# Four graph layers on one core: the sage layer's products moved behind the second layer's sums

## The chip, the cores and the metric

The kernel runs on one core of one Trainium2 chip. The metric is the device time of one execution in microseconds (us), and a lower time is better. The engines are named as in the profile: PE is TensorE (PEld its weight loads), DVE is VectorE, ACT is ScalarE, POOL is GpSimd, SP is SyncE, which here only starts transfers.

## The reference, cut to what matters

Eight graphs (B = 8) of N = 2048 nodes with F = 128 features go through four layers. Each layer is fed h, the normalised and rectified x, and its result is added to x.

```python
# layer 0: graph attention, 8 heads, then a second attention layer over its result
att = softmax(where(adj > 0, leaky_relu(f1_i + f2_j), NEG)); xc = elu(att @ h)      # 8 heads
att2 = softmax(where(adj > 0, leaky_relu(g1_i + g2_j), NEG)); x = x + elu(att2 @ (xc @ W2)) + h
# layer 1 ("sage"): the greatest feature of each node's neighbours
h = relu(layernorm(x))
neigh_agg = where(mask[..., None], h[:, None], -1e30).max(axis=2)                   # h itself where there is none
o = h @ W_self + b_self + neigh_agg @ W_neigh + b_neigh
x = x + relu(layernorm(o) * gamma + beta)
# layer 2: graph attention with 4 heads ("gat_mid"); layer 3: a mean over neighbours and two products
```

## The kernel before, in words

Nodes lie in T = 16 tiles of 128 partitions. One graph after the other goes through the stages, but two graphs are in flight, since the sage layer's maxima need a gather that takes long. For graphs b = 0 to 7 the order, written out by hand in `pipeline`, is: load and heads of 0; `beside(0, None)`; load and heads of 1; then six times `beside(b + 1, b)`, `middle(b)`, `last_layer(b, b + 2)`, `heads_of(b + 2)`; then `beside(7, 6)`, `middle(6)`, `last_layer(6)`, `beside(None, 7)`, `middle(7)`, `last_layer(7)`. Every engine runs its own program through the same order and waits on semaphores.

`heads_of` is layer 0's first attention (8 heads, LA). `beside(b, other)` holds two things: the second attention layer of graph b (LB), and the sage layer of the graph before it (other = b - 1). `middle` is layer 2 (LC) and `last_layer` is layer 3, beside which the next graph is loaded.

The gather of graph b is POOL's: it fetches rows of a table in memory by lists of neighbours (`table`, one indirect transfer for each of 8 neighbours of a tile, line 552), keeps the greatest (lines 535 to 538), and writes `Agg` (line 596). It starts when SP has stored h of graph b as the table (line 452), which SP does after norm 1, and after the gather of graph b - 1 has ended (the semaphore `maxima`, line 614). The table store of graph b thus needs, in this order: LB's preparation (`prepare`), its sums (`sums` on PE, line 1386, fed by DVE's products of line 908 through `weigh`), the second layer's `finish` on DVE (nine operations, lines 991 to 1007, with an exponential on ACT between, `elu_exp`), `statistics(1)` on DVE, and norm 1 on ACT (line 635, 16 instructions).

The sage layer of the graph before stands in the same stage. PE first waits for `maxima` (`sage_arrived`). For each of 8 pairs of tiles PE turns four blocks (lines 1343 and 1344), ACT copies them (line 718, `sage_operands`), PE multiplies (line 1355), and DVE adds the row of biases (line 1180, `sage_sums`) and takes statistics (line 1187). These steps stand between the 16 steps of LB's sums: after step 1 PE runs `sage_arrived`, and steps 2 to 9 have a product each behind them. When they are done, norm 4 (ACT), `joined` (DVE, three operations and `statistics(2)`) and norm 2 (ACT) follow, then DVE's `finish`. The list of one tile of neighbours (three parts of `list_tile`: lines 1053, 1077, 1067) is also made between steps 0 to 2 of the sums.

A few lines say it best, on PE and on DVE:

```python
for jb in range(T):                                  # sums, PE
    ...
    ins.then_inc(s["pe"], 1)
    if other is not None:
        sage_step(other, jb)                         # jb == 1: waits for maxima
...
if other is not None:                                # beside, DVE, after weigh(...)
    joined(other)
if b is not None:
    finish(LB, b, lone)
    statistics(1, b, X)
```

Of the kernel before, what the change touches and what calls it, by code (L numbers as in the profile page):

```python
# [31 lines left out]
ACT = mybir.ActivationFunctionType  # L32
# [31 lines left out]
def build(nc, x, adj, W1, a1, W2, a2, Wself, bself, Wneigh, bneigh, gamma, beta, WC, aC, W3, B3, out):  # L64
    B, N, F = x.shape
    T = N // P
    LA = Layer("gat_heads", W1.shape[0], W1.shape[2], 1)
    LB = Layer("gat_out", 1, F, W1.shape[0] * W1.shape[2] // P)
# [16 lines left out]
    with ExitStack() as ctx:  # L85
# [182 lines left out]
        def plain(eng):  # L268

            eng.wait_ge(ready, 1)  # L270
# [355 lines left out]
        def _(act):  # L626
# [84 lines left out]
            def sage_operands(b):  # L711

                s = M["sage"]
                with act.Fori(0, T // 2) as tt:
                    plain(act)
                    act.wait_ge(s["T"], b * T + tt * 2 + 2)
                    act.wait_ge(s["W"], b * T + tt * 2 + 2)
                    act.activation(hT[:, :, :, :], ps[:, 6, :].rearrange("p (u k c) -> p u k c", u=2, k=2),  # L718
                                   ACT.Copy).then_inc(s["hT"], 2)
# [60 lines left out]
            def beside(b, other):  # L780
                if b is not None:
                    prepare(LB, b)
                if other is not None:
                    sage_operands(other)
                    norm(4, other, Y, Y, ACT.Identity)
                    norm(2, other, X2, Hn2, ACT.Relu)
                if b is not None:
                    elu_exp(LB, b, 0)
                    norm(1, b, X, Hn, ACT.Relu)
# [40 lines left out]
        def _(dve):  # L830
# [148 lines left out]
            def finish(L, hn, lone):  # L979

                s, C = S[L], L.C
                v = Chain(dve, s["pv"], (hn + 2) * POST[L], POST[L])
# [13 lines left out]
                v(dve.tensor_tensor(Z[:, full * w:], Z[:, full * w:], ps[:, full, 0:T * C - full * w], ALU.add))  # L996
                v(dve.reciprocal(rden[:, :], zt[:, :, L.D]))
                v(dve.tensor_tensor(o, o, rden[:, :].rearrange("p (t o) -> p t o", o=1).broadcast_to([P, T, L.D]), ALU.mult))
                v(dve.tensor_scalar(E, o, 0.0, None, ALU.min))
                plain(dve)  # L1000
                dve.wait_ge(s["e"], hn + 1)
                v(dve.scalar_tensor_tensor(E, o, 0.0, E, ALU.max, ALU.add))

                plain(dve)
                dve.wait_ge(h0_in, hn * 16 + 16)
                v(dve.scalar_tensor_tensor(Hn[:, :, :], E, -1.0, Hn[:, :, :], ALU.add, ALU.add))
                v(dve.tensor_tensor(X[:, :, :], X[:, :, :], Hn[:, :, :], ALU.add))
                v.end()

# [173 lines left out]
            def sage_statistics(b, p):  # L1183
                plain(dve)
                dve.wait_ge(M["sage"]["ev"], b * T + (2 * p + 4))
                for t in (2 * p, 2 * p + 1):
                    dve.bn_stats(stats[:, t, :], Y[:, t, :]).then_inc(ln[4]["st"], 1)

            def beside(b, other):

                rest_of = []
                between = [] if other is None or b is None else list(zip((0, 1, 2), list_tile(b, LIST_LB)))
                if other is not None:
                    for p in range(T // 2):
                        between.append((p + 4, lambda p=p: sage_sums(other, p)))
                        between.append((p + 5, lambda p=p: sage_statistics(other, p)))
                    between.append((T // 2 + 4, lambda: rest_of.append(deviations(4, other))))
                    between.append((T // 2 + 5, lambda: rest_of[0]()))
                if b is None:
                    for at, work in sorted(between, key=lambda part: part[0]):  # L1200
                        work()
                else:
                    prepare(LB, b)
                    weigh(LB, 0, (b + 1) * 16, slice(0, 1), b, between)
                if other is not None:
                    joined(other)
                if b is not None:
                    finish(LB, b, lone)


                    statistics(1, b, X)

# [67 lines left out]
        def _(pe):  # L1280
# [83 lines left out]
            def sage_step(b, jb):  # L1364

                if jb == 1:
                    sage_arrived(b)
                if 2 <= jb < T // 2 + 2:
                    sage_product(b, jb - 2)
                if 1 <= jb < T // 2 + 1:  # L1370
                    sage_turned(b, jb - 1)

            def sums(L, hn, other):

                s = S[L]
                if other is not None:

                    plain(pe)
                    pe.wait_ge(s["hsc"], hn + 1)
                for jb in range(T):  # L1380
# [8 lines left out]
                    if other is not None:  # L1389
                        sage_step(other, jb)  # L1390
# [109 lines left out]
            def beside(b, other):  # L1500
                if b is None:
                    for jb in range(T // 2 + 2):
                        sage_step(other, jb)
                    return
                prepare(LB, b, xc, None)
                plain(pe)
                pe.wait_ge(S[LB]["v"], (b + 1) * PREP_CHAIN)
                sums(LB, b, other)
# [36 lines left out]
```

## Time and profile before

| | us |
|---|---|
| median of 3 runs | 9122.6 (9110.27 to 9135.99) |
| the profiled execution's own time | 9111.52 |
| its span, first to last instruction | 9109.8 |
| busy: DVE, PE, POOL, PEld, ACT | 5894.4, 5148.5, 5128.1, 4779.8, 4402.1 |
| mean granted TensorE clock, as a share of full speed | 0.781 |

Busy time is the sum of an engine's instructions; a share over the whole span mixes stages with different limits. A row of a timeline gives start, duration, engine, line, operation, operands and in brackets how long the engine had been idle and what ended that. "x16" means that sixteen like instructions in a row are merged. A row of stretches gives for each engine the busy time and in parentheses the number of instructions.

### The profile page before, as it was taken

How to read it: one execution, taken by the hardware profiler on the slowest of the kernel's cores; microseconds unless marked ns; L12 is line 12 of the kernel's file. 1: busy time of each engine (PE TensorE's matmuls, PEld its weight loads, DVE VectorE, ACT ScalarE, POOL GpSimd, SP SyncE). 2: the span in 40 equal slices, each digit the busy share in tenths (PEclk: the TensorE clock that was granted, in tenths of full speed). 3: DMA queues.
4: the chain of work that ended last, by engine and by line, in shares of the span. 5: the costliest groups of instructions: out<-in, count | busy, mean ns of one | idle time of the engine just before them, and what ended most of it. 6: DMA issues, size and time to landing. Idle time of an engine off the chain costs nothing.

```text
span 9109.8 us, 178961 instructions
## 1 busy us (share of the span) xinstructions
PE 5148.5 (57%) x60584; PEld 4779.8 (52%) x60584; DVE 5894.4 (65%) x7002; ACT 4402.1 (48%) x3608; POOL 5128.1 (56%) x5234
## 2 busy tenths in 40 slices
PE   3673750365765668365865667556845667362026
PEld 3672750364755557363865567555745567361025
DVE  5874860386867788486867687687847688581024
ACT  5644730165635566165735566356715566160034
POOL 0004777377764677377764677276764677377630
PEclk9885875687877878687987888788877888686568
DMA  2114332234332533135322433234322433132210
GB/s 99 43 34 124 66 66 25 46 69 113 61 63 65 122 65 80 19 76 133 67 62 66 119 66 83 58 75 101 69 48 66 120 65 80 54 55 58 23 26 29
DMA packets 307180, 629.05 MB, mean 69 GB/s; under 512 B 113553, under 2 KB 165906, under 8 KB 270610
## 3 DMA queue, kind: packets, MB, share of 16 engines
q0 software_dynamic: 91936, 161.87, 16.9%
q1 hardware_dynamic: 212354, 456.38, 14.2%
q8 instruction: 581, 9.52, 0.4%
q14 instruction: 149, 1.22, 0.0%
q10 hardware_dynamic: 2160, 0.06, 0.0%
HBM read 506.89 MB, written 111.15 MB: 68 GB/s over the span
## 4 chain that ended last, share of the span: by engine, by line
POOL 20%; issue 16%; DVE 14%; PE 13%; DMA 8%; ACT 4%; POOLq 2%; DVEq 2%; ACTq 1%; SPq 0%
DMA G<-table,idx 6%; POOL G L552 6%; POOL best L552 5%; PE ps L1413 4%; POOL best L538 4%; PE ps L1386 3%; PE ps L1415 2%; POOL best L535 2%; DVE keys L1077 2%; POOL G L535 2%; ACT Pbuf L689 1%; PE ps L1438 1%; DVE key L1067 1%; POOL best L537 1%; ACT Hn L689 1%
## 5 line engine op out<-in xcount | busy, mean ns | idle before, releaser
L552 POOL DMA_INDIRECT G<-table,idx x1416 | 1502.7, 1061 | 508.5 <-issue 452.7
L1415 PE MATMUL ps<-Hn,AT 128*128 128x99 bf16 x12288 | 1774.5, 216 | 0.0
L1415 PE MATMUL ps<-X,AT 128*128 128x99 bf16 x12288 | 1735.0, 214 | 52.6 <-issue 52.6
L544 POOL DMA_DIRECT2D idx<-lists x433 | 259.3, 599 | 2445.9 <-issue 1964.9
L689 ACT ACTIVATE Hn<-Rb,q 128x2048 int8<-128x2048 f32 x768 | 1485.4, 1988 | 86.6 <-PE ps L1415 82.1
L689 ACT ACTIVATE Pbuf<-Rb,q 128x2048 int8<-128x2048 f32 x768 | 1487.8, 1987 | 18.2 <-PE ps L1415 15.6
L552 POOL DMA_INDIRECT best<-table,idx x1024 | 1093.7, 1068 | 319.4 <-issue 309.3
L1415 PEld LDWEIGHTS ps<-X,AT 128*128 128x128 fp8e4 x12288 | 1243.2, 101 | 57.6 <-issue 57.6
L1415 PEld LDWEIGHTS ps<-Hn,AT 128*128 128x128 fp8e4 x12288 | 1256.5, 102 | 0.0
L1413 PE MATMUL ps<-X,Hn 128*128 128x198 bf16 x6144 | 933.6, 268 | 567.6 <-DVE Hn L937 358.6
L1413 PE MATMUL ps<-Hn 128*128 128x198 bf16 x6144 | 960.3, 272 | 433.0 <-DVE Zs L957 236.0
L1413 PEld LDWEIGHTS ps<-X,Hn 128*128 128x128 fp8e4 x6144 | 650.4, 106 | 594.0 <-issue 578.1
L1413 PEld LDWEIGHTS ps<-Hn 128*128 128x128 fp8e4 x6144 | 659.8, 107 | 474.5 <-issue 454.4
L1413 PE MATMUL ps<-Hn,Pbuf 128*128 128x198 bf16 x6144 | 833.9, 252 | 75.9 <-DVE Pbuf L937 75.6
L1413 PE MATMUL ps<-X,Pbuf 128*128 128x198 bf16 x6144 | 821.9, 251 | 28.7 <-DVE Pbuf L937 28.7
L908 DVE SCALAR_TENSOR_TENSOR Pbuf<-Rb,q,AT 128x2048 f32<-128x2048 f32 x128 | 303.7, 2374 | 803.0 <-PE ps L1386 781.7
L937 DVE SCALAR_TENSOR_TENSOR Hn<-Hn,AT 128x512 int32<-128x512 int32 x768 | 638.7, 860 | 219.3 <-ACT Hn L689 155.4
L718 ACT ACTIVATE hT<-ps 128x512 f32<-128x512 f32 x64 | 38.2, 597 | 1515.8 <-PE ps L1344 1515.8
L937 DVE SCALAR_TENSOR_TENSOR Pbuf<-Pbuf,AT 128x512 int32<-128x512 int32 x768 | 668.0, 899 | 137.7 <-ACT Pbuf L689 104.7
L1077 DVE MAX8 keys<-key 128x8 f32<-128x2056 f16 x305 | 701.2, 2299 | 33.8 <-DVE key L1067 7.8
L1343 PE MATMUL ps<-ident,Hn 128*128 128x128 f32 x128 | 34.5, 293 | 1146.3 <-POOLq L614 1096.9
L1413 PEld LDWEIGHTS ps<-Hn,Pbuf 128*128 128x128 fp8e4 x6144 | 606.9, 99 | 89.3 <-issue 86.9
(186 smaller groups left out, 11171.7 us busy)
## 6 DMA issues: line engine op xcount, KB each, us to landing
Rb<-in_adj SPq DMA_DIRECT2D x128, 1024.0 KB, 6.3
Rb<-rrows SPq DMA_DIRECT2D x104, 1024.0 KB, 6.3
bytes_A<-A SPq DMA_DIRECT2D x128, 256.0 KB
bytes_AT<-AT SPq DMA_DIRECT2D x128, 256.0 KB
AT<-bytes_AT SPq DMA_DIRECT2D x128, 256.0 KB, 3.6
AT<-bytes_A SPq DMA_DIRECT2D x128, 256.0 KB, 4.6
G<-table,idx POOLq DMA_INDIRECT x1416
h<-Hn SPq DMA_DIRECT2D x16, 1024.0 KB, 4.1
```

Source lines behind the costliest of these rows:

```text
L535: v(pool.tensor_tensor(b, b, a, ALU.subtract))
L537: v(pool.tensor_scalar(b, b, 3.0e38, 0.0, ALU.min, ALU.max))
L538: v(pool.tensor_tensor(a, a, b, ALU.add))
L544: pool.dma_start(idx[:, slot, :], lists[bass.ds(r, 1)].rearrange("o p k -> (o p) k")).then_inc(idx_in[slot], 16)
L552: pool.indirect_dma_start(out=dst[:, k, :], out_offset=None, in_=table, in_offset=bass.IndirectOffsetOnAxis(ap=idx[:, slot, k:k + 1], axis ...
L689: act.activation(marks[(u * T + jb) % RING].bitcast(I8), Rb[:, u, :], ACT.Sign, bias=q[:, jb, hs], scale=-1.0).then_inc(s["sg"], 1)
L908: dve.scalar_tensor_tensor(tiles_P[jb % 2], Rb[:, slot, :], q[:, jb, h], AT[:, jb, :], ALU.max, ALU.mult).then_inc(s["p"], 1)
L937: dve.scalar_tensor_tensor(marks[k % RING], marks[k % RING], NO_SIGN, A32, ALU.bitwise_and, ALU.bitwise_and).then_inc(s["p"], 1)
L1077: dve.max(keys8[:, :], key[:, :]).then_inc(found, 1)
L1386: ins = pe.matmul(ps[:, i // L.per_bank, c0:c0 + L.width], tiles_P[jb % 2][:, i * P:(i + 1) * P], rhs, start=(jb == 0 and i % L.per_bank = ...
L1413: pe.matmul(both[:, :, 0:G], greater[:, at], v.rearrange("p (g x) -> p g x", g=2), start=first, stop=False, skip_group_check=True)
L1415: ins = pe.matmul(both[:, 0, 0:G], A8[:, jb, at], v[:, 0:G], start=False, stop=jb == T - 1, skip_group_check=True)
```

## The change

On PE the sage layer's steps leave the loop of LB's sums and follow it as a block of their own, `sage`, which waits for the maxima and then turns and multiplies pair after pair. On DVE, `finish` gets a list `between`: after its third operation and after each later one it takes one `sage_sums` out of the list. The sage statistics are no longer taken pair by pair; `statistics(4)` takes them together, after `statistics(1)`, and `joined` comes last. On ACT the eight copies stand around the second layer's exponential, four ahead of it and four behind, then norm 1, then norm 4 and norm 2. The copies are written out where they were a loop. The list of a tile is made behind steps 1 to 3 in place of 0 to 2. SP's program is as before.

```diff
 act:
-            def sage_operands(b):
-                with act.Fori(0, T // 2) as tt:
+            def sage_operands(b, part):
+                for p in part:
...
                 if b is not None:
                     prepare(LB, b)
                 if other is not None:
-                    sage_operands(other)
+                    sage_operands(other, range(T // 4))
+                if b is not None:
+                    elu_exp(LB, b, 0)
+                if other is not None:
+                    sage_operands(other, range(T // 4, T // 2))
+                if b is not None:
+                    norm(1, b, X, Hn, ACT.Relu)
+                if other is not None:
                     norm(4, other, Y, Y, ACT.Identity)
                     norm(2, other, X2, Hn2, ACT.Relu)
-                if b is not None:
-                    elu_exp(LB, b, 0)
-                    norm(1, b, X, Hn, ACT.Relu)
 dve:
-            def finish(L, hn, lone):
+            def finish(L, hn, lone, between):
+                waiting = list(between)
+                def beside_it():
+                    if waiting:
+                        waiting.pop(0)()
...
                 v(dve.tensor_tensor(Z[:, full * w:], Z[:, full * w:], ps[:, full, 0:T * C - full * w], ALU.add))
+                beside_it()
                 v(dve.reciprocal(rden[:, :], zt[:, :, L.D]))
+                beside_it()
...
                 v(dve.tensor_tensor(X[:, :, :], X[:, :, :], Hn[:, :, :], ALU.add))
+                beside_it()
                 v.end()
+                while waiting:
+                    beside_it()
...
+                products = [] if other is None else [lambda p=p: sage_sums(other, p) for p in range(T // 2)]
...
                     prepare(LB, b)
-                    weigh(LB, 0, (b + 1) * 16, slice(0, 1), b, between)
+                    weigh(LB, 0, (b + 1) * 16, slice(0, 1), b,
+                          () if other is None else list(zip((1, 2, 3), list_tile(b, LIST_LB))))
+                    finish(LB, b, lone, products)
+                    statistics(1, b, X)
                 if other is not None:
+                    plain(dve)
+                    dve.wait_ge(M["sage"]["ev"], other * T + (T + 2))
+                    statistics(4, other, Y)
                     joined(other)
-                if b is not None:
-                    finish(LB, b, lone)
-                    statistics(1, b, X)
 pe:
-            def sage_step(b, jb):
-                if jb == 1:
-                    sage_arrived(b)
-                if 2 <= jb < T // 2 + 2:
-                    sage_product(b, jb - 2)
-                if 1 <= jb < T // 2 + 1:
-                    sage_turned(b, jb - 1)
+            def sage(b):
+                sage_arrived(b)
+                for p in range(T // 2):
+                    sage_turned(b, p)
+                    sage_product(b, p)
...
                     ins.then_inc(s["pe"], 1)
-                    if other is not None:
-                        sage_step(other, jb)
...
-                sums(LB, b, other)
+                sums(LB, b)
+                if other is not None:
+                    plain(pe)
+                    pe.wait_ge(S[LB]["hsc"], b + 1)
+                    sage(other)
```

## Rows read from the trace of the kernel before

**Rows 1.** Waits, longest in total: us in total, times, longest.

```profile
PE ps L1343 <- POOLq L614: 1096.9, 6, 463.0
```

**Rows 2.** Stretches from the end of a gather to the next table store.

```profile
1676.00:1790.60 114.60, 65.39 (x554) 64.81 (x555) 69.63 (x101) 34.22 (x65) 0.00 (x0) 0.77 0.00 2
2704.00:2818.30 114.30, 65.12 (x554) 64.54 (x555) 69.63 (x101) 34.23 (x65) 0.00 (x0) 0.77 0.00 2
3754.90:3869.40 114.50, 65.31 (x554) 64.73 (x555) 69.63 (x101) 34.23 (x65) 0.00 (x0) 0.77 0.00 1
4747.50:4862.40 114.90, 65.63 (x554) 65.05 (x555) 69.64 (x101) 34.22 (x65) 0.00 (x0) 0.77 0.01 2
5708.00:5833.00 125.00, 66.89 (x561) 65.87 (x561) 83.54 (x111) 34.22 (x65) 0.00 (x0) 0.77 0.01 1
6797.80:6913.20 115.40, 66.15 (x554) 65.57 (x555) 69.62 (x101) 34.23 (x65) 0.00 (x0) 0.77 0.01 2
7819.50:7937.80 118.30, 65.56 (x554) 65.05 (x555) 69.65 (x101) 34.21 (x65) 0.00 (x0) 0.76 0.00 1
```

**Rows 3.** Stretches, middle to second layer's sums; last: one where PE waits.

```profile
1825.30:2647.00 821.70, 559.16 (x6912) 515.98 (x6912) 642.22 (x730) 507.51 (x375) 588.83 (x588) 0.83 0.40 82
2854.10:3661.20 807.10, 555.77 (x6911) 512.96 (x6911) 638.08 (x726) 508.05 (x374) 576.94 (x575) 0.84 0.38 83
3904.30:4694.80 790.50, 557.56 (x6912) 513.89 (x6912) 632.56 (x714) 507.19 (x375) 578.32 (x576) 0.84 0.40 85
4896.90:5698.20 801.30, 555.51 (x6912) 511.88 (x6912) 624.20 (x726) 506.60 (x375) 581.02 (x580) 0.84 0.37 84
5867.70:6690.30 822.60, 562.75 (x6912) 518.21 (x6912) 649.85 (x738) 507.02 (x375) 584.58 (x579) 0.83 0.39 82
6947.60:7759.10 811.50, 558.16 (x6912) 514.99 (x6912) 634.32 (x718) 507.10 (x375) 583.87 (x585) 0.84 0.38 83
1313.00:1676.00 363.00, 0.76 (x7) 0.57 (x6) 15.34 (x10) 0.00 (x0) 258.65 (x298) 0.51 0.24 25
```

**Rows 4.** Timeline of the first handover, 1676 to 1826 us.

```profile
1676.48 0.47 PE L1343 MATMUL ps<-ident,Hn 128*128 128x128 f32 x1 [362.73 <-POOLq L614]
...
1753.63 2.31 DVE L991 TENSOR_TENSOR Pbuf<-lone,hsum 128x2064 f32<-128x2064 f32 x1 [0.18 <-DVE small L858]
...
1769.13 2.29 DVE L1007 TENSOR_TENSOR X<-X,Hn 128x2048 f32<-128x2048 f32 x1
...
1782.17 7.31 ACT L635 ACTIVATE Hn<-X,small  x16 [0.91 <-DVE small L858]
...
1790.63 0.83 SPq L452 DMA_DIRECT2D table<-Hn  x1
...
1804.08 2.36 DVE L892 TENSOR_TENSOR WHbuf<-WHbuf,d 128x2112 f32<-128x2112 f32 x1
...
1818.22 0.71 DVE L923 TENSOR_TENSOR Zs<-WHbuf,q 128x528 f32<-128x528 f32 x1 [11.78 <-DMA AT<-bytes_AT]
...
1825.28 7.66 ACT L689 ACTIVATE Hn<-Rb,q 128x2048 int8<-128x2048 f32 x4
```

**Rows 5.** Timeline of the last sage layer, which runs alone.

```profile
8754.63 0.45 PE L1343 MATMUL ps<-ident,Hn 128*128 128x128 f32 x1 [462.98 <-POOLq L614]
...
8775.53 0.43 DVE L1180 TENSOR_TENSOR xcbuf<-ps,rowsb 128x256 f32<-128x256 f32 x1 [1.33 <-PE ps L1355]
...
8779.43 7.18 ACT L635 ACTIVATE xcbuf<-xcbuf,small  x16 [1.05 <-DVE small L858]
```

**Rows 6.** Timeline rows of the second layer's sums, in three graphs.

```profile
634.31 59.91 PE L1386 MATMUL ps<-WHbuf,Pbuf 128*128 128x129 f32 x512 [5.18 <-DVE Pbuf L908]
...
4712.21 2.35 DVE L908 SCALAR_TENSOR_TENSOR Pbuf<-Rb,q,AT 128x2048 f32<-128x2048 f32 x1 [0.39 <-DVE found_idx L1082]
...
5721.23 4.62 DVE L908 SCALAR_TENSOR_TENSOR Pbuf<-Rb,q,AT 128x2048 f32<-128x2048 f32 x2 [0.38 <-DVE found_idx L1082]
...
5723.73 6.24 PE L1386 MATMUL ps<-WHbuf,Pbuf 128*128 128x129 f32 x32 [8.45 <-DVE Pbuf L908]
```

More of the change, by code:

```diff
@@ L709, in heads @@
                     elu_exp(LA, b * LA.H + LA.H - 1, LA.H - 1)
-            def sage_operands(b):
+            def sage_operands(b, part):
                 s = M["sage"]
-                with act.Fori(0, T // 2) as tt:
+                for p in part:
                     plain(act)
-                    act.wait_ge(s["T"], b * T + tt * 2 + 2)
-                    act.wait_ge(s["W"], b * T + tt * 2 + 2)
+                    act.wait_ge(s["T"], b * T + (p * 2 + 2))
+                    act.wait_ge(s["W"], b * T + (p * 2 + 2))
                     act.activation(hT[:, :, :, :], ps[:, 6, :].rearrange("p (u k c) -> p u k c", u=2, k=2),
@@ L1002, in finish @@
                 v(dve.scalar_tensor_tensor(E, o, 0.0, E, ALU.max, ALU.add))
+                beside_it()
                 plain(dve)
@@ L1006, in finish @@
                 v(dve.scalar_tensor_tensor(Hn[:, :, :], E, -1.0, Hn[:, :, :], ALU.add, ALU.add))
+                beside_it()
                 v(dve.tensor_tensor(X[:, :, :], X[:, :, :], Hn[:, :, :], ALU.add))
+                beside_it()
                 v.end()
+                while waiting:
+                    beside_it()
             def heads(L, b, lone, lists=None):
@@ L1181, in sage_sums @@
                                   rowsb[:, 0:1, :].broadcast_to([P, 2, F]), ALU.add).then_inc(M["sage"]["ev"], 2)
[L1183 to L1187, printed above, removed]
-            def beside(b, other):
-                rest_of = []
-                between = [] if other is None or b is None else list(zip((0, 1, 2), list_tile(b, LIST_LB)))
-                if other is not None:
[L1194 to L1198, printed above, removed]
+            def beside(b, other):
+                products = [] if other is None else [lambda p=p: sage_sums(other, p) for p in range(T // 2)]
                 if b is None:
-                    for at, work in sorted(between, key=lambda part: part[0]):
+                    for work in products:
                         work()
@@ L1362, in sage_arrived, with sums @@
                 pe.wait_ge(x1_in, (b + 1) * 32)
-            def sage_step(b, jb):
-                if jb == 1:
-                    sage_arrived(b)
-                if 2 <= jb < T // 2 + 2:
-                    sage_product(b, jb - 2)
-                if 1 <= jb < T // 2 + 1:
-                    sage_turned(b, jb - 1)
-            def sums(L, hn, other):
+            def sage(b):
[3 more added lines that the diff above has]
+                    sage_product(b, p)
+            def sums(L, hn):
                 s = S[L]
-                if other is not None:
-                    plain(pe)
-                    pe.wait_ge(s["hsc"], hn + 1)
                 for jb in range(T):
@@ L1388, in sums @@
                     ins.then_inc(s["pe"], 1)
-                    if other is not None:
-                        sage_step(other, jb)
             def head(L, hn, u):
@@ L1501, in beside @@
                 if b is None:
-                    for jb in range(T // 2 + 2):
-                        sage_step(other, jb)
+                    sage(other)
                     return
@@ L1507, in beside @@
                 pe.wait_ge(S[LB]["v"], (b + 1) * PREP_CHAIN)
-                sums(LB, b, other)
+                sums(LB, b)
+                if other is not None:
+                    plain(pe)
+                    pe.wait_ge(S[LB]["hsc"], b + 1)
+                    sage(other)
             def middle(b, alone):
```

## The prediction

> **What bounds the kernel now.** I read the waits first, then the stretches around the point where one gather ends and the next begins, then the timeline of one such point. PE waits 1096.9 us in six places for the semaphore with which POOL reports a gather's end, 463.0 us of it in the last [rows 1]. So the gather is late wherever PE reaches it. The stretches from a gather's end to the next table store, seven of them, are 114.3 to 125.0 us long, and POOL does nothing in them (0.00, x0) [rows 2]. The gathers fill the time between: from table store to end they take 2704.0 - 1790.6 = 913.4, then 936.6, 878.1, 845.6, 964.8, 906.3 and, from 7937.8 to 8754.6, 816.8 us [rows 2, 5]. From the first end (1676.0) to the last (8754.6) pass 7078.6 us, and this is a plain loop: gather, handover, gather.
>
> The other engines have a loop of their own through the same point. From the first mark of the middle layer (1825.3) to the first step of the next second-layer sums (2647.0) pass 821.7 us, then 807.1, 790.5, 801.3, 822.6, 811.5 [rows 3]. Then they wait: sums begin at 2647.0 and the gather ends at 2704.0, so 57.0 us, and likewise 93.7, 52.7, 9.8, 107.6 and 60.4 us in the five stages after [rows 2, 3]. In the fourth of them the two loops are almost level. This slack is what the change can use up, and no more.
>
> **The handover after the change.** Only the sage products and `finish` stand between a gather's end and the statistics that lead to the table. Where the sage layer runs alone, its eight products are evicted 8775.53 + 0.43 - 8754.63 = 21.3 us after PE goes on [rows 5]. `finish` takes 1771.42 - 1753.63 = 17.8 us by itself [rows 4]. Both run on DVE in turns: the least is 21.3 (`finish` fits between the products), the most 39.1 (no overlap). DVE has only 8 x 0.43 us of the products, the rest of their time is spent on PE and ACT, so the value lies near the low end; since `finish`'s exponential now stands between ACT's fourth and fifth copy and delays the fifth product, I take 26. From `finish`'s end to norm 1's start pass 1782.17 - 1771.42 = 10.75 us, and the table store is issued 1790.63 - 1782.17 = 8.46 later [rows 4], together 19.2. The change adds waits for the products on DVE. Queued behind them are the rest of `finish`, statistics(1), and so norm 1 and the table store; all of these stood behind the maxima before too, so nothing new is held by a late gather. So the table goes out 26 + 19.2 = 45.2 us after the gather's end, where it now takes 114.3 to 125.0 [rows 2]. SP's program is the same; its two stores ahead of the table are in the 8.46.
>
> The gather also loses quiet time. In 363.0 us in which the others stand still POOL runs 298 instructions, 0.821 per us; in 821.7 loaded us 588, 0.716 per us [rows 3]: the same work takes 14.7% longer. A gather's end now ran quiet for 10 to 108 us, of which the first 20 or so hold the list of a tile; 14.7% of the rest is 0 to 13 us. I add 8 us to each gather but the last, whose end is quiet in both kernels. The bounds are 0 and 13.
>
> The Trainium skill says that GpSimd shares its SBUF interfaces with VectorE and contends with Vector instructions that have two SBUF inputs (GPSIMD Engine Reference, section 8, Key points). The trace agrees: 0.821 against 0.716 instructions per us [rows 3]. If that rule alone held, the move of more two-input DVE work beside the gather would speak against the change; it is the rival "slower gather" below.
>
> **The other loop after the change.** From the same release: 26 us to `finish`'s end. Then statistics(1) 10.75, statistics(4) another 10.75 (norm 1's 7.31 runs on ACT beside it), norm 4 7.3, `joined`'s three operations 3 x 2.33 = 7.0, statistics(2) 10.8, norm 2 7.3; then the middle layer's preparation as before, 1806.44 - 1789.48 = 17.0; then the first splits and the first mark, 1825.28 - 1818.22 = 7.1 [rows 4]. The sum behind `finish` is 78.0; with 1.4 for a gather that now runs beside it, 79.4. Before, DVE stood 11.78 us for AT ahead of the splits, which began 1818.22 - 1790.63 = 27.6 us after the table store that SP issues ahead of AT's transfers [rows 4]. Now 70.9 - 19.2 = 51.7 us lie between the two, so this wait is covered; if it is not, it costs up to 11.8 a stage. The release thus stands 26 + 79.4 = 105.4 us ahead of the first mark, where it was 1825.3 - 1676.0 = 149.3 [rows 3].
>
> What this loop gains there it pays at the sums. They cost little of it now, since they ran after the gather's end; they now stand wholly ahead of the products. In two graphs, begun at 4694.8 and 5698.2, DVE's product for step 3 started 17.4 and 23.0 us later, behind one and two further rounds of the list [rows 3, 6]. With the list one step later, one more product (2.3) comes ahead: step 4 can start some 22.2 and 27.8 us after the first. Then twelve steps on PE: the first after a stall 6.24, the others (59.91 - 6.24) / 15 = 3.58 each [rows 6], 45.6 in all. So 67.8 and 73.4, mean 70.6, and 0.8 until DVE is as far as it is in the late-gather case (`finish`'s first three operations against PE's first product). The least is 59.9, with the list hidden [rows 6]; the most has every step at 6.24, below.
>
> A turn of the gather's loop is now 45.2 + 8 + gather, of the other loop 105.4 + 71.4 + stretch of rows 3. The longer one counts:
>
> | to end of gather | gather's loop | other loop | taken | before |
> |---|---|---|---|---|
> | 1 | 966.6 | 998.5 | 998.5 | 1028.0 |
> | 2 | 989.8 | 983.9 | 989.8 | 1050.9 |
> | 3 | 931.3 | 967.3 | 967.3 | 992.6 |
> | 4 | 898.8 | 978.1 | 978.1 | 960.5 |
> | 5 | 1018.0 | 999.4 | 1018.0 | 1089.8 |
> | 6 | 959.5 | 988.3 | 988.3 | 1021.7 |
> | 7 | 862.0 | none | 862.0 | 935.1 |
>
> The sums are 6802.0 after and 7078.6 before: 276.6 us less. The last sage layer loses its interleaved statistics: norm 4 began 8779.43, and will begin 8775.96 + 10.75 = 8786.7, 7.3 later [rows 5]. The first graphs, up to 1676.0, are as before; the unrolled copies on ACT and the register work for DVE's added waits are costed at nothing, since the waits for PE cover them (at 0.2 us each, uncovered, 1.6 a stage). Net 276.6 - 7.3 = 269 us. The profiled execution's own 9111.5 becomes 8842; the median before is 11.1 above that execution, so from 9122.6 I forecast 8850 us.
>
> **Rivals.** *The sums are hidden anyway* (the other loop never binds): all seven turns by the gather's loop sum to 6626, 453 less, or 8677 us. For it: the loop has slack in every stage. Against it: each slack shrinks by the 69 us that the handover gives up and the 71 that the sums take, and gets back 44 at the mark and 8 from the longer gather, so by 88; of the six only 93.7 and 107.6 outlast that.
>
> *The sums run at the lower clock.* PE comes to them after pauses, and such a step takes 6.24, not 3.58; the granted clock is 0.51 where PE waits and 0.83 in loaded stretches [rows 3, 6]. All twelve steps at 6.24 cost 29.3 more, and the second column's turns sum to 6953 with the last: 9005 us. Against it: the sixteen steps of the first graph, also begun after a pause, take 59.91, or 3.74 each on average [rows 6]. The Trainium skill has TensorE at 1.2 GHz after idleness and at 2.4 GHz after sustained activity (TensorE: Matmul & The Clock Gate, Part 1); by it, too, only the beginning is slow.
>
> *Slower gather.* If the gather, with DVE busy at all times beside it, takes 10% more, the turns sum to 7207 and the time is 9258 us. The point from which it decides is 7% to 8%: at 7% the time is about 9096, at 8% 9150, where it becomes slower. For it: 14.7% between quiet and loaded. Against it: the gathers are loaded for most of their length already.
>
> *Nothing moves.* `finish` still waits for the maxima through its first product, so the table can't be stored before they are there; if the turns of DVE, PE and ACT wait for each other at every product, the handover stays near 115 and the time near 9123. Against it: 39.1 us is the sum of both without any overlap.
>
> **Chances.** Forecast 0.75, hidden sums 0.07, lower clock 0.06, slower gather 0.07, nothing moves 0.05. A measurement of this kernel can tell about 0.3%, 27 us, from no change. Faster by that: 0.88; within it 0.05; slower 0.07. The forecast's own range: `finish` at 21.3 and sums at 59.9 give some 80 less, `finish` at 39.1 in seven handovers 92 more, so 8770 to 8943. Leaving out hidden sums, slower gather and nothing moves (0.19), the range reaches to the lower clock: 8770 to 9010.
>
> **What would show it.** In the profile after, the gather's end to the table store should take about 45 us where the gather is late and PE's wait for it should fall from 1096.9 to about 770: some 300 in the first, 440 in the last, and the rest in one or two between. Of the middle five handovers, three or four should have PE not waiting at all, with the maxima 10 to 90 us before the end of the sums. The sums should take 68 to 74 from first to last step, the first mark should follow the release by about 105, and the gathers should be 0 to 13 us longer. I am wrong if the stretches of rows 3 change by more than 1%, if the handover is above 60, or if a gather is over 3% longer.

## The result, and the profile after

The changed kernel takes 8874.44 us (median of 4, 8863.03 to 8889.48) where the kernel before takes 9119.47 beside it: a ratio of 0.972, 95% interval 0.969 to 0.975. The forecast was 8850, its range 8770 to 9010. The profiled execution after took 8871.89, its span is 8870.2, so 239.6 less than the span before, where the prediction's sum has 269 less. The change does what was forecast; in the profiles, 30 us of the gain are missing.

The page after, first lines (engine, busy us, share of the span, instructions):

```profile
span 8870.2 us, 179248 instructions
...
PE 5220.8 (59%) x60584; PEld 4827.2 (54%) x60584; DVE 5925.3 (67%) x7002; ACT 4381.6 (49%) x3594; POOL 5220.3 (59%) x5234
```

Its waits (us in total, times, longest), to be read beside [rows 1]:

```profile
DVE xcbuf L1199 <- PE ps L1364: 841.7, 49, 452.1
...
PE ps L1352 <- POOLq L614: 770.9, 3, 453.2
```

PE's wait for the maxima falls from 1096.9 us in six places to 770.9 in three, which is the forecast's 770. That the sum fits so closely is luck in part: the first gather's wait is 311.9 (some 300 were forecast), the last one's 453.2 (440), and the one between them 5.8 (30). DVE's 841.7 us for the sage products are no new bound: 768 of them are these same three waits, since DVE waits behind PE.

The stretches from a gather's end to the next table store, in the columns of [rows 2]:

```profile
1687.70:1730.30 42.60, 14.68 (x96) 12.36 (x96) 24.81 (x56) 15.49 (x27) 0.00 (x0) 0.74 0.01 2
2637.10:2738.30 101.20, 67.43 (x519) 64.42 (x517) 64.54 (x76) 15.50 (x27) 0.00 (x0) 0.81 0.01 2
3682.90:3732.10 49.20, 23.70 (x96) 20.20 (x96) 24.79 (x56) 15.61 (x27) 0.00 (x0) 0.50 0.01 3
4646.20:4706.40 60.20, 33.02 (x224) 30.14 (x222) 36.49 (x62) 15.61 (x27) 0.00 (x0) 0.73 0.01 2
5534.40:5683.80 149.40, 98.06 (x710) 93.05 (x710) 94.21 (x116) 22.20 (x41) 0.00 (x0) 0.75 0.05 17
6654.60:6700.90 46.30, 17.95 (x110) 15.40 (x109) 29.66 (x59) 15.49 (x27) 0.00 (x0) 0.71 0.01 3
7623.00:7669.30 46.30, 17.17 (x96) 14.70 (x96) 26.04 (x57) 15.50 (x27) 0.00 (x0) 0.65 0.00 2
```

Two kinds stand here. Four handovers are 42.6 to 49.2 us long: the gather is late, or within some 5 us of the end of the sums, and only products, `finish`, statistics(1) and norm 1 stand behind it. In the second, fourth and fifth POOL is done first and waits until the sums end, in the fifth for 101.7 us. There PE's instruction count (x710) shows what it is still doing: all of the sums. This is the other loop. The third is the longest of the four late ones: over it, after a pause of PE of 5.75 us, the granted clock is 0.50, the lower of the two levels, and PE's 96 instructions take 23.70 us. The first, after a pause of 311.9, has 0.74 and 14.68; why the two differ is not shown. Before, the handovers stood at 0.76 to 0.77 [rows 2], with the sums between the products.

The second layer's sums, from their first step to their last:

```profile
2624.00:2692.90 68.90, 63.26 (x514) 62.72 (x515) 47.35 (x24) 0.00 (x0) 11.83 (x10) 0.91 0.01 1
3604.70:3677.60 72.90, 61.30 (x512) 60.68 (x512) 54.08 (x28) 0.00 (x0) 59.21 (x42) 0.90 0.17 22
4594.80:4660.40 65.60, 61.14 (x514) 60.79 (x515) 45.96 (x24) 0.00 (x0) 43.91 (x29) 0.95 0.10 13
5564.40:5636.10 71.70, 61.56 (x514) 61.21 (x515) 49.61 (x29) 0.00 (x0) 0.00 (x0) 0.90 0.01 1
6581.60:6656.20 74.60, 62.27 (x514) 61.73 (x515) 54.26 (x29) 0.00 (x0) 60.08 (x44) 0.91 0.10 15
7553.00:7619.40 66.40, 61.80 (x512) 61.28 (x512) 46.88 (x24) 0.00 (x0) 54.76 (x38) 0.94 0.10 17
```

They take 65.6 to 74.6 us, at a granted clock of 0.90 to 0.95, so near the upper of the two levels. Call the later of the gather's end and the end of the sums the release. The first handover after its release, in the timeline:

```profile
1688.19 0.47 PE L1352 MATMUL ps<-ident,Hn 128*128 128x128 f32 x1 [311.92 <-POOLq L614]
...
1692.22 0.42 DVE L1199 TENSOR_TENSOR xcbuf<-ps,rowsb 128x256 f32<-128x256 f32 x1 [311.08 <-PE ps L1364]
...
1721.86 7.32 ACT L635 ACTIVATE Hn<-X,small  x16 [0.93 <-DVE small L862]
...
1730.34 0.84 SPq L452 DMA_DIRECT2D table<-Hn  x1
1732.11 7.16 ACT L635 ACTIVATE xcbuf<-xcbuf,small  x16 [0.96 <-DVE small L862]
...
1790.39 3.88 ACT L689 ACTIVATE Hn<-Rb,q 128x2048 int8<-128x2048 f32 x2
```

Norm 1 starts 34 us after the release, the table goes out at 42.6, and norm 4 of the sage layer (the second L635 row) runs behind it; the middle layer's first mark (L689) follows at 102.7. From there to the next sums, in the columns of [rows 3]:

```profile
1790.40:2624.00 833.60, 565.04 (x6912) 520.31 (x6912) 656.35 (x730) 506.81 (x375) 599.15 (x606) 0.82 0.38 81
2799.10:3604.70 805.60, 558.30 (x6911) 514.67 (x6911) 638.97 (x726) 507.27 (x375) 579.93 (x584) 0.84 0.38 83
...
5745.10:6581.60 836.50, 555.64 (x6911) 512.72 (x6911) 656.50 (x738) 507.44 (x375) 601.52 (x599) 0.83 0.39 81
```

All six are 833.6, 805.6, 802.7, 797.0, 836.5 and 792.5 us, +11.9 to -19.0 against [rows 3] and 13 us more in sum.

Where the 239.6 us come from follows from the ends of the gathers (1687.7, 2637.1, 3682.9, 4646.2, 5534.4, 6654.6, 7623.0, 8504.4) and the table stores between them, measured in both profiles and set beside the prediction's terms:

| part of the span | before | after | change | predicted |
|---|---|---|---|---|
| up to the first gather's end | 1676.0 | 1687.7 | +11.7 | 0 |
| seven stretches from gather to table | 817.0 | 495.2 | -321.8 | -324.6 |
| seven gathers, table to end | 6261.6 | 6321.5 | +59.9 | +48 |
| behind the last gather | 355.2 | 365.8 | +10.6 | +7.3 |
| sum | 9109.8 | 8870.2 | -239.6 | -269.3 |

This follows the gather alone. Where the sums end last, a longer gather only shortens the wait in the next stretch, so a row here is not yet a cost.

### The profile page after: what moved, and what is told of

It is laid out like the page before. It is cut to its first block and busy times, and to the rows that moved or that the text cites. A ratio compares the mean times of both kernels' runs of the same rounds, so it can differ in the third digit from the quotient of the medians.

```text
span 8870.2 us, 179248 instructions
## 1 busy us (share of the span) xinstructions
PE 5220.8 (59%) x60584; PEld 4827.2 (54%) x60584; DVE 5925.3 (67%) x7002; ACT 4381.6 (49%) x3594; POOL 5220.3 (59%) x5234
## 5 line engine op out<-in xcount | busy, mean ns | idle before, releaser
L1416 PE MATMUL ps<-X,AT 128*128 128x99 bf16 x12288 | 1742.1, 215 | 48.2 <-issue 48.2
L689 ACT ACTIVATE Hn<-Rb,q 128x2048 int8<-128x2048 f32 x768 | 1484.7, 1987 | 89.6 <-PE ps L1416 86.0
L689 ACT ACTIVATE Pbuf<-Rb,q 128x2048 int8<-128x2048 f32 x768 | 1487.8, 1987 | 15.1 <-PE ps L1416 11.9
L552 POOL DMA_INDIRECT best<-table,idx x1024 | 1130.0, 1104 | 318.2 <-issue 309.0
L941 DVE SCALAR_TENSOR_TENSOR Pbuf<-Pbuf,AT 128x512 int32<-128x512 int32 x768 | 644.8, 868 | 147.4 <-ACT Pbuf L689 114.8
L1414 PEld LDWEIGHTS ps<-X,Pbuf 128*128 128x128 fp8e4 x6144 | 601.9, 98 | 30.1 <-issue 29.5
L1439 PE MATMUL ps<-WHbuf,AT 128*128 128x385 bf16 x2048 | 390.1, 352 | 351.3 <-ACT WHbuf L813 351.3
```

Source lines behind the costliest of these rows:

```text
L552: pool.indirect_dma_start(out=dst[:, k, :], out_offset=None, in_=table, in_offset=bass.IndirectOffsetOnAxis(ap=idx[:, slot, k:k + 1], axis ...
L689: act.activation(marks[(u * T + jb) % RING].bitcast(I8), Rb[:, u, :], ACT.Sign, bias=q[:, jb, hs], scale=-1.0).then_inc(s["sg"], 1)
L941: dve.scalar_tensor_tensor(marks[k % RING], marks[k % RING], NO_SIGN, A32, ALU.bitwise_and, ALU.bitwise_and).then_inc(s["p"], 1)
L1414: pe.matmul(both[:, :, 0:G], greater[:, at], v.rearrange("p (g x) -> p g x", g=2), start=first, stop=False, skip_group_check=True)
L1416: ins = pe.matmul(both[:, 0, 0:G], A8[:, jb, at], v[:, 0:G], start=False, stop=jb == T - 1, skip_group_check=True)
L1439: ins = pe.matmul(ps[:, 4 + u, 0:3 * F + 1], A8[:, k, (tt * 2 + u) * P:(tt * 2 + u + 1) * P], PS3[:, k, 0:3 * F + 1], start=k == 0, stop=k ...
```

## The experiments

The first theory is that of the prediction: two loops meet at the release, and both parts of the change are needed, the early table for the gather's loop and the sums ahead for the other. The rivals: one part alone brings it all; what counts is that products and `finish` alternate, or that they do not; and, for the missing 30 us, either the stages' own work or a gather held up by DVE. Each ratio is to the kernel before, beside it on the same chip.

**The early table alone.** On the kernel before, the sage layer stays between the steps of the sums; only the order behind them changes.

```diff
-                if other is not None:
-                    joined(other)
                 if b is not None:
                     finish(LB, b, lone)
                     statistics(1, b, X)
+                if other is not None:
+                    joined(other)
```

ACT has norm 2 behind norm 1 to match.

> The kernel before with only the order changed behind the sums: finish, statistics(1) and norm 1 come ahead of joined and norm 2; the sage steps stay between the steps of the sums. Two-loop theory (the turns are set by the gather with its handover, or by the other engines' loop with the sums, whichever is longer): the handover falls from 114.6 to about 100 (63.3 of sums, 17.8 of finish, 19.2 to the table), seven times 14 us, so about 9020 us against 9119. Rival (the gain comes only from the second layer's sums no longer waiting for the maxima): no change, 9119.

9084.87 us, ratio 0.995 (0.992 to 0.997). The first handover:

```profile
1676.80:1777.50 100.70, 63.45 (x544) 63.26 (x544) 64.39 (x81) 25.65 (x46) 0.00 (x0) 0.81 0.01 2
```

The handovers shorten as expected, to about 100 us (124.3 in the fifth), 88 us less in seven. But the gathers take 44 us more in sum (6305.4 against 6261.6) and the stretch behind the last one 8, so the span is only 36 us shorter where 100 were expected, though here not one step of the sums has moved ahead of a gather's end. Work that stood in the handover, where POOL is idle, now runs beside the next gather. The prediction gave this nothing.

**The sums ahead alone.** On the changed kernel, the table again comes last.

```diff
                     finish(LB, b, lone, products)
-                    statistics(1, b, X)
                 if other is not None:
                     ...
                     statistics(4, other, Y)
                     joined(other)
+                if b is not None:
+                    statistics(1, b, X)
```

ACT has norm 4 and norm 2 ahead of norm 1.

> The changed kernel with joined, norm 4 and norm 2 put back ahead of statistics(1) and norm 1; the sums still stand ahead of the sage products. Two-loop theory: the handover grows from about 45 to about 81 (statistics, norm 4 and joined come into it), the other loop gets about 10 shorter; the turns then are mostly the gather's and the time is about 8980. Rival (only the sums' place counts): 8874, as the changed kernel. Together with e1 this splits the gain: 100 us for the table alone, 140 for the sums alone, 245 for both.

9054.44 us, 0.991 (0.988 to 0.994).

```profile
1690.10:1771.00 80.90, 21.17 (x106) 17.50 (x107) 38.61 (x86) 31.53 (x63) 0.00 (x0) 0.56 0.00 1
```

DVE's waits for AT, before and here (the changed kernel has none):

```profile
DVE Zs L923 <- DMA AT<-bytes_AT: 78.7, 7, 12.1
```

```profile
DVE Zs L927 <- DMA AT<-bytes_AT: 75.4, 7, 13.3
```

Where the gather is late the handover is 81 to 84 us, as expected; the release to the first mark is 115 to 120 us, not the 95 expected. Norm 1 now stands ahead of the middle layer's copies on ACT, which begin 79 to 83 us behind the release (77 to 84 in the changed kernel), so the 10 us are not gained. And the wait for AT is back, 10.8 us a stage, since SP issues AT's transfers behind the table store, which again goes out late: an early table also covers this wait. The time is some 74 us above the 8980 expected. So the parts alone bring 0.5% and 0.9%, together 2.8%: more than their sum. That one part brings it all is refuted. Its gathers, 6360.8 us in sum, are longer than in either kernel; why, these runs don't tell.

**No turns.** All eight products ahead of `finish`.

```diff
-                    finish(LB, b, lone, products)
+                    for work in products:
+                        work()
+                    finish(LB, b, lone, ())
```

ACT has all eight copies ahead of `elu_exp`.

> The changed kernel with all eight sage_sums ahead of the first operation of finish, and all eight copies ahead of the exponential. Two-loop theory: 21.3 us of products and 17.8 of finish then stand one behind the other, about 39 in place of 24 to 31, in both loops, so seven turns of about 12 us: 8960. Rival (the products' round trips set that stretch whatever stands between them): 8874.

8971.64 us, 0.982 (0.980 to 0.984), so 1% more than the change.

```profile
3706.40:3765.50 59.10, 15.47 (x96) 13.06 (x96) 30.00 (x59) 15.61 (x27) 0.00 (x0) 0.66 0.01 2
```

The release to `finish`'s end takes 36.8 to 40 us (48.2 in the first), near the prediction's bound without overlap of 39.1, where the changed kernel takes 24.0 to 30.6. The seven turns take 11 us more on average, 77 of the 90 us by which the span is longer (8960.0 against 8870.2). The rival, for which 8874 would stand, is refuted.

**Longer sums.** Behind each product DVE takes one more maximum, whose result nobody uses.

```diff
+                    if jb < T:
+                        dve.max(hpart[:, 136 + 8 * jb:144 + 8 * jb], iota[:, :])
```

> The changed kernel with one more DVE operation of about 2.3 us (a maximum over one tensor, whose result nobody reads) behind each of the 16 products of the sums, so that the sums take about 19 us more. Two-loop theory: 13 to 26 us more in each of the six turns of the loop (the slack there is at most 15), about 100 in all, so about 8978. Rival (the sums are hidden behind the gather): 8874.

9002.19 us, 0.984 (0.978 to 0.990).

```profile
1317.60:1408.40 90.80, 65.46 (x512) 62.99 (x512) 86.78 (x44) 0.00 (x0) 74.00 (x53) 0.89 0.16 18
```

The sums take 83.6 to 95 us, 15 to 20 more, and the span is 115 us longer: 25 up to the first gather's end, where two graphs' sums are longer too, and 90 in the turns. Five of the first six turns are 15 to 23 us longer; the fifth, for which 13 to 26 were expected too, only 0.9. So the sums are on the path, and the rival that they are hidden anyway is refuted.

**A shorter gather.** The last comparison over the eight neighbours is left out.

```diff
-                for width in (4, 2, 1):
-                    greater(v, best[:, 0:width, :], best[:, width:2 * width, :])
+                pool.sem_inc(tree, TREE - 1)
+                v.n = TREE - 1
```

> The changed kernel whose gather leaves out the last comparison over the eight columns (nine operations of POOL for each tile, about 7.5 us, so about 120 to 130 us a graph); Agg then holds the first column only. Two-loop theory: only the first gather, the last one and two turns that are level gain, about 260 us, so about 8610. Rival (the gather sets every turn): all eight gathers gain, about 1000 us, so about 7870.

8483.36 us, 0.927 (0.922 to 0.932); the profile's span is 393 us below the change's. The two loops as I had put them gave 8610, so the gain is some 127 us larger than that; the gather setting every turn would have given 7870. From the first mark to the next sums:

```profile
1668.20:2462.40 794.20, 554.23 (x6912) 511.68 (x6912) 617.50 (x730) 506.92 (x375) 489.98 (x471) 0.84 0.40 85
2632.50:3420.50 788.00, 553.02 (x6911) 510.90 (x6911) 608.80 (x726) 506.13 (x375) 509.53 (x488) 0.84 0.42 87
...
5513.60:6319.00 805.40, 554.43 (x6911) 512.04 (x6911) 627.00 (x738) 506.88 (x375) 517.13 (x502) 0.84 0.42 85
```

The gathers are 123 to 155 us shorter each, and in all six stages between, the sums now end 119 to 207 us behind the gather. So the other loop alone sets the turns there, and only the first gather (the first mark comes at 1668.2, not 1790.4) and the last count in full: 122 + 130 us. The remainder is the surprise: the other loop's stretches are shorter too, 130 us in sum. DVE runs the same 730 instructions in 617.50 us instead of 656.35, with 22% fewer POOL instructions beside it (471 against 606). So POOL slows DVE.

**A product with one input.** The second layer's product leaves out the factor AT and so reads one tensor in place of two; one takes 1.29 us in place of 2.35.

```diff
-                    dve.scalar_tensor_tensor(tiles_P[jb % 2], Rb[:, slot, :], q[:, jb, h], AT[:, jb, :],
-                                             ALU.max, ALU.mult).then_inc(s["p"], 1)
+                    dve.tensor_scalar(tiles_P[jb % 2], Rb[:, slot, :], q[:, jb, h], 1.0,
+                                      ALU.max, ALU.mult).then_inc(s["p"], 1)
```

> The changed kernel whose product for the second layer's sums reads one tensor in place of two (the mask AT is left out of it). In the changed kernel's trace a POOL operation that meets such a product takes about 2 us more, and gathers that end beside the sums are about 18 us longer there. If it is the second tensor that holds POOL up: POOL runs about 0.8 instructions per us beside the sums in place of 0.58 to 0.62, and the time falls by 20 to 40 us. If any DVE work does: the rate stays near 0.6.

8814.03 us, 0.963 (0.958 to 0.968). The first graph's sums beside the gather, in the change and here:

```profile
1301.60:1376.30 74.70, 61.54 (x512) 60.80 (x512) 54.15 (x28) 0.00 (x0) 59.50 (x46) 0.89 0.18 22
1376.30:1687.00 310.70, 0.00 (x0) 0.00 (x0) 4.76 (x3) 0.00 (x0) 221.38 (x255) 0.51 0.23 24
```

```profile
1306.60:1377.30 70.70, 62.16 (x512) 61.79 (x512) 39.13 (x28) 0.00 (x0) 54.03 (x50) 0.90 0.23 24
```

In the change POOL runs 46 instructions in 74.7 us, 0.616 per us, and behind the sums 255 in 310.7, 0.821. With the shorter product it is 50 in 70.7, 0.707. I had expected 0.8 if only a second tensor counts and 0.6 if the number of inputs does not matter. It is between, and the timeline shows why:

```profile
7519.56 0.94 POOL L552 DMA_INDIRECT best<-table,idx  x1 [0.30 <-issue]
7520.81 1.47 POOL L552 DMA_INDIRECT best<-table,idx  x1 [0.30 <-issue]
...
7520.88 2.48 DVE L912 TENSOR_SCALAR Pbuf<-Rb,q 128x2048 f32<-128x2048 f32 x2 [0.38 <-PE ps L1389]
```

The issue of a transfer that begins 0.07 us ahead of the first of two products lasts 1.47 us instead of 0.94. It is held by a product with one input as well, but for a shorter time. The span is 52 us shorter than the change's, more than the 20 to 40 expected: the gathers are 48 us shorter in sum, and the sums, too, are shorter, at 61.5 to 71.9 us.

**The list ahead of the sums.** Two of the list's three parts are run ahead of `prepare(LB, b)`.

```diff
+                    parts = () if other is None else list_tile(b, LIST_LB)
+                    for work in parts[:2]:
+                        work()
                     prepare(LB, b)
-                          () if other is None else list(zip((1, 2, 3), list_tile(b, LIST_LB))))
+                          () if other is None else [(1, parts[2])])
```

> The changed kernel with the first two parts of the tile's list (keys, first round) made ahead of the second layer's preparation, where DVE stands for about 5 us anyway; only the further rounds stay in the sums, behind step 1. Two-loop theory: the sums get 6 to 8 us shorter, which counts in the turns of the other loop alone (four of seven), so about 8850. Rival (the gather sets every turn, the sums are hidden): 8874.

8892.55 us, 0.974 (0.972 to 0.976): a miss, nothing gained. DVE in the pause behind the heads, in the change:

```profile
2599.25 0.43 DVE L872 COPY WHbuf<-ps 128x256 f32<-128x256 f32 x1 [6.01 <-PE ps L1322]
```

The same here, and the sums:

```profile
2591.94 2.29 DVE L1072 SCALAR_TENSOR_TENSOR key<-A,iota 128x2048 f16<-128x2048 uint8 x1 [3.03 <-issue]
...
2598.57 0.43 DVE L872 COPY WHbuf<-ps 128x256 f32<-128x256 f32 x1 [0.24 <-DVE found_idx L1101]
```

```profile
2624.40:2685.20 60.80, 60.56 (x515) 60.37 (x516) 40.28 (x20) 0.00 (x0) 15.87 (x12) 0.95 0.01 1
```

The sums do shrink, here from 68.90 to 60.80, in all graphs by 1.4 to 8.1. But the stretch ahead of them, from DVE's last operation of the heads, grows by 0.4 to 10.5 us in six of the seven graphs. The list does not fit into DVE's pause of 6.0 us: it begins 3.0 us into it, runs for 6.4 and so delays the evictions behind it (L872). The list is moved, not hidden.

**Statistics beside the products, and the list spread out.** The first variant takes the sage statistics pair by pair, each behind the next product, in a buffer of its own, so that only the last pair stands behind statistics(1).

```diff
...
+            def sage_part(b, p):
+                sage_sums(b, p)
+                if p:
+                    sage_statistics(b, p - 1)
...
```

> The changed kernel with the sage statistics taken pair by pair again, each behind the next product, into a buffer of their own; behind statistics(1) only the short end of them stays. Two-loop theory: statistics(4) gives back 7.8 us of the other loop, and the pairs put 1 to 4 us into the handover; that counts in the four turns that the other loop sets, so 15 to 20 us less in all, about 0.2%. Rival (the gather sets the turns): the handover's 1 to 4 us alone, 0.1% to 0.3% slower.

The second also puts the parts of the list behind steps 2, 6 and 10 of the sums in place of 1, 2 and 3.

> As the one before, and the three parts of the tile's list behind steps 2, 6 and 10 of the sums in place of 1, 2 and 3, so that PE's steps of 3.58 us against DVE's 2.35 take up part of each. Two-loop theory: the sums fall from 66 to 75 us to about 62 to 68, so another 5 us in four turns, together 30 to 40 us less than the changed kernel, 0.4%. Rival (the gather sets the turns): no faster than the changed kernel.

The change was measured again on the same chip.

> The changed kernel once more, to compare these two with it on one chip: 0.972 of the kernel before.

8863.29 us (0.972, 0.969 to 0.975) and 8874.82 (0.972, 0.970 to 0.974), where the change itself gives 8912.83 (0.975, 0.972 to 0.977). These intervals overlap. Set against the change's own five runs, the means (8873 and 8874 us against 8905) are 31 us or 0.35% lower, with 95% intervals of 4 to 59 and 10 to 51 us: a small gain, in the direction that was expected. But it is not shown to come from what was expected. In one profile of each, the release to the first mark is no shorter with the first variant (108.7 to 110.6 us; 105.7 to 111.2 in the change), and the second does not have its shorter sums (67.3 to 76.6 us). The stretches from first mark to sums, which neither variant touches, are 44 and 51 us shorter in sum. The change's profile is the slowest of its five runs and theirs are among the fastest, so this may be chance in part; why stays open.

## Why the prediction was right

**Two loops through one release: right.** Of the prediction's last column, the turns from release to release came out so:

| | 1 | 2 | 3 | 4 | 5 | 6 | 7 |
|---|---|---|---|---|---|---|---|
| predicted | 998.5 | 989.8 | 967.3 | 978.1 | 1018.0 | 988.3 | 862.0 |
| measured | 1005.2 | 990.0 | 977.5 | 975.7 | 1020.1 | 966.8 | 881.4 |

The sum is 6816.7 against 6802.0, closer than the turns themselves: +19.4 in the last and -21.5 in the sixth cancel, and that is luck. Turns 1, 3 and 4 ended with the sums, 55.8, 14.2 and 101.7 us behind the gather, and turns 2 and 7 with the gather, as the table names them. Turns 5 and 6 came out level, within 1.6 and 3.7 us, each decided by the loop that the table does not name. The longer sums, the shorter gather and the two half changes show the mechanism from both sides, though the times of all four missed what was expected of them by 24 to 127 us.

**The terms at the release: right.** `finish` and products 24.0 to 30.6 us (26 taken, 39.1 without turns, which the run without them confirms), the table 42.6 to 49.2 behind the release (45.2), the first mark 102.7 to 109.2 (105.4), the sums 65.6 to 74.7 (67.8 and 73.4). The covered wait for AT stays covered. What the prediction did not look at here is the clock of the sage products: they now stand behind a pause of PE, and where the granted clock of a whole handover was 0.50 (the third, three when the change was run again, the first of the run without turns) `finish` and products came out at the long end, at 30.6 in the third.

**The gathers: mechanism right, two terms put at nothing.** The step that was off is "I add 8 us to each gather but the last, whose end is quiet in both kernels", with "the first graphs, up to 1676.0, are as before". The 8 us themselves came out in sum only: the six gathers before the last are 41.6 us longer, against 48, but singly they differ by -17.6 to +36.0, and only two lie in the 0 to 13 that I had given. The last gather is 18.3 us longer (835.1 against 816.8), the first one's end comes 11.7 later, and I had put both at nothing. On both the gather sets the time, so they count in full. The missing 30 us are thus 11.7 up to the first gather's end, 19.4 in the last turn, and 3.3 behind the last gather (10.6, not 7.3); the six turns before the last take 4.7 less than predicted. What stands behind the two:
- The first gather has the second graph's sums beside it now, ahead of its end: 46 POOL instructions in 74.7 us, 0.616 per us against 0.821 when the sums are over, so the same work takes 33% longer. I had left this out. Beside the sums of the other graphs the rate goes down to 0.572 (38 in 66.4 us), 43% longer, where I had 14.7% from the 0.716 of a loaded stage.
- The rest of the handover's work, moved behind the table store, runs beside the next gather. The early table alone, with no sums moved, shows this: +44 us in seven gathers, some 9 of them in the last. The last gather of the changed kernel also has this work beside it; where the rest of its 18.3 us comes from was not tried.

**The six stretches, and one gather: outside the bounds that I had named.** "I am wrong if the stretches of rows 3 change by more than 1%" came true in four of six (1.4% to 2.3%, three up and one down), and the third gather is 4.1% longer (914.1 against 878.1) where I had set 3%. In sum both nearly cancel, 13 us for the stretches and 1.0% for the gathers, so the time stood. The pattern returned when the change was run again (836.6, 805.6, 801.3, 806.5, 833.9, 787.6), so it is no chance; the third gather took 902.9 there, 2.8% more. A gather whose beginning and end fall elsewhere in a stage holds DVE elsewhere, and the shorter gather shows that POOL's work does lengthen such a stretch; that this makes the pattern, stage by stage, was not tried.

**The rivals.** *Hidden sums* is refuted by the longer sums. *The lower clock* did not come in the sums (0.90 to 0.95), but it did in the third handover (0.50), where no rival looked for it. *Slower gather* was the right mechanism at about a seventh of the size at which it would have decided: the gathers are 1.0% longer, not 7%.

## What to carry to other kernels

When two loops meet at one wait, work out a turn of each and take the longer at each place; a change that helps one loop is worth its slack against the other, and here each half alone gave a third of both or less. Work that is moved out of a stretch in which an engine stands idle lands beside that engine's own work: look at the rate next to the very instructions that it will meet, too, and not only at a mean over a stage. When costing such a move, list every stage in which the neighbour changes, the first and the last too: here the mean served well enough for six gathers in sum, and the two that were left out make up the error.

## What the runs showed of the hardware

The price of DVE and POOL side by side was not expected at this size, nor that it holds in both directions. In the changed kernel, POOL's rows and DVE's in one stretch:

```profile
3626.38 0.94 POOL L552 DMA_INDIRECT G<-table,idx  x1 [0.30 <-issue]
3627.63 0.95 POOL L552 DMA_INDIRECT G<-table,idx  x1 [0.31 <-issue]
3628.60 1.27 POOL L535 TENSOR_TENSOR G<-G,best 128x512 f32<-128x512 f32 x1
...
3630.77 3.18 POOL L538 TENSOR_TENSOR best<-best,G 128x512 f32<-128x512 f32 x1
...
3646.62 2.01 POOL L552 DMA_INDIRECT G<-table,idx  x1 [0.30 <-issue]
3648.94 0.94 POOL L552 DMA_INDIRECT G<-table,idx  x1 [0.30 <-issue]
```

```profile
3622.86 0.17 DVE L1101 CAST found_idx<-keys 128x8 uint32<-128x8 f32 x1 [0.21 <-DVE keys L1096]
...
3626.03 2.30 DVE L1096 MAX8 keys<-key 128x8 f32<-128x2056 f16 x1
3628.54 1.37 DVE L1101 CAST found_idx<-keys 128x8 uint32<-128x8 f32 x1 [0.21 <-DVE keys L1096]
3630.29 2.53 DVE L912 SCALAR_TENSOR_TENSOR Pbuf<-Rb,q,AT 128x2048 f32<-128x2048 f32 x1 [0.38 <-DVE found_idx L1101]
3632.75 3.35 DVE L912 SCALAR_TENSOR_TENSOR Pbuf<-Rb,q,AT 128x2048 f32<-128x2048 f32 x1
...
3645.46 2.35 DVE L912 SCALAR_TENSOR_TENSOR Pbuf<-Rb,q,AT 128x2048 f32<-128x2048 f32 x1 [1.29 <-PE ps L1389]
3649.03 2.35 DVE L912 SCALAR_TENSOR_TENSOR Pbuf<-Rb,q,AT 128x2048 f32<-128x2048 f32 x1 [1.22 <-PE ps L1389]
```

The product at 3645.46 runs until 3647.81. The transfer's issue that begins at 3646.62 lasts 2.01 us and ends 0.82 behind the product, nearly the whole length that it needs alone (0.94). It is held until the product ends, not slowed in proportion. The issue at 3648.94, begun 0.09 ahead of the next product, takes its 0.94, and that product its 2.35: neither holds the other. This is regular in the trace. Of 32 issues that begin inside such a product 30 end 0.81 to 0.89 us behind it; the two others, begun 0.06 and 0.09 into one, and all 25 begun 0.01 to 0.62 ahead of one take 0.94 to 1.01. With the product of one input it is not so: there all seven issues begun 0.06 to 0.33 ahead take 1.47 to 1.74 and end 0.12 behind the product. So such an issue looks to need something of DVE's at two points, near its beginning and near its end, and the product with two inputs holds it at the first alone; this is an inference from these ends.

POOL's arithmetic is held too, and holds in turn. L538 at 3630.77, begun inside a product that runs until 3632.82, takes 3.18 us, where the same form takes 1.26 in a quiet stretch; the next product, from 3632.75, takes 3.35 in place of 2.35, past L538's end at 3633.95. Of the 128 products 23 take over 2.55 us in the changed kernel, and 3 before. DVE's small conversion takes 0.17 us alone. The one at 3628.54 began inside the issue of 3627.63, waited for its end and for that of the L535 behind it, and took 1.37, both ending at about 3629.9; each of the 25 conversions of 0.85 us or more ends 0.03 to 0.04 us behind an operation of POOL's L535 or L538. Beside the maximum of 2.30 us (MAX8) the issue at 3626.38 is not held.

The Trainium skill has this rule (SBUF — State Buffer, "SBUF: two separate sides"): the port pair that DVE and GpSimd share is an exclusive lock, whichever starts first keeps it for its whole instruction, and the other blocks. It names DVE operations with two SBUF inputs (against a GpSimd operation that reads SBUF) or in a 2-port mode. The trace agrees where POOL comes second to the product with two inputs (2.01 against 0.94 us) and where such a product comes second to L538 (3.35 against 2.35). That the issue at 3648.94 and the product behind it did not hold each other, and that L535 went ahead of a conversion whose recorded start is 0.06 us earlier, is not told by that rule alone. That the shorter product with one input held POOL too (1.47 us), and that the conversion waits, would fit the second of the page's conditions; no run here shows in which mode they ran.
